# Late fused weights, scaled plain weights beside the experts, and other cyclic orders in a two-layer cross-attention and MoE kernel

## The reference, cut to what matters

```python
# layer 0
x = x + cross_attention(layernorm(x), ctx)            # 16 heads of 16, masked
xn = layernorm(x)
probs = softmax(xn @ w_switch + b_switch); e = argmax # 8 experts, one per token
keep = (position of the token in its expert) <= 512   # capacity
x = x + gate * (relu(xn_e @ w1[e] + b1[e]) @ w2[e] + b2[e])
# layer 1
h = cross_attention with biases (layernorm(x), ctx); ffn W1, W2 ; h = x + ...
nodes[-1] = layernorm(h)
for c in 0..5:                                        # a cell of six attention nodes
    q, k, v = (src @ We[edge]) * ew[c] @ Wq/Wk/Wv[c]  # 8 heads of 32
    nodes[c] = nodes[c-1] @ We[edge] * ew + attention(q, k, v) @ Wo[c] * act_w[c]
out = h + layernorm(nodes[5]) * ln_g + ln_b
```

## Time and profile before

| | |
|---|---|
| median of 3 runs | 4257.91 us (4254.85 to 4258.33) |
| the profiled execution's own time | 4261.87 us |
| its span | 4260.1 us |
| mean granted TensorE clock | 0.978 |
| PE busy | 4052.2 us, 95% |
| DVE, ACT, POOL busy | 59%, 62%, 42% |

### The profile page before, as it was taken

How to read it: one execution, slowest core, us unless ns; L and a number is a source line. 1 busy time by engine, 2 the same in 40 slices (tenths; PEclk the granted TensorE clock), 3 DMA queues, 4 the chain that set the end, 5 groups by cost and what they waited for, 6 DMA issues and landing times.

```text
span 4260.1 us, 100693 instructions
## 1 busy us (share of the span) xinstructions
PE 4052.2 (95%) x38276; PEld 3431.3 (81%) x38276; DVE 2515.5 (59%) x6280; ACT 2647.2 (62%) x11818; POOL 1774.9 (42%) x1883
## 2 busy tenths in 40 slices
PE   8889998995999999999999999999999999999997
PEld 7778876664788888888888888888888888888885
DVE  6778883103566666566666666566666666666553
ACT  7778881112666666666666666666666666666663
POOL 4566662002344444444444444444444444444332
PEclk9999998997999999999999999999999999999998
DMA  4122214321000000000000000000000000000000
GB/s 161 55 66 74 63 52 140 110 71 51 14 14 14 14 14 13 13 13 14 20 15 14 14 13 12 12 12 12 12 12 12 12 12 19 11 14 11 4 4 6
DMA packets 117867, 129.75 MB, mean 30 GB/s; under 512 B 12006, under 2 KB 110676, under 8 KB 117264
## 3 DMA queue, kind: packets, MB, share of 16 engines
q1 hardware_dynamic: 105648, 109.80, 8.2%
q0 software_dynamic: 6144, 8.43, 0.7%
q10 hardware_dynamic: 5600, 5.07, 0.4%
HBM read 89.68 MB, written 41.94 MB: 31 GB/s over the span
## 4 chain that ended last, share of the span: by engine, by line
PE 58%; DVE 9%; ACT 5%; POOL 3%; issue 1%; DMA 0%; SPq 0%; POOLq 0%; DVEq 0%
PE c_product L1297 26%; PE c_product L1308 12%; PE c_product L1348 8%; PE c_scores L1338 6%; ACT c_front_probs L1118 4%; PE c_product L1371 4%; DVE c_neg_max L1173 2%; DVE c_xn L1158 2%; DVE c_routed L1158 1%; PE c_product L1359 1%; DVE c_x L1183 1%; POOL c_rstd L1064 1%; ACT c_probs L1118 1%; POOL c_probs L1076 1%; PE c_product L1285 1%
## 5 line engine op out<-in xcount | busy, mean ns | idle before, releaser
L1118 ACT ACTIVATE c_probs<-c_scores,c_neg_max 128x128 f32<-128x128 f32 x3072 | 1081.9, 407 | 480.5 <-DVE c_neg_max L1173 480.5
L1076 POOL TENSOR_TENSOR c_probs<-c_probs,c_row_inv 128x512 f32<-128x512 f32 x768 | 790.5, 1041 | 1211.3 <-DVE c_row_inv L1176 1208.7
L1297 PE MATMUL c_product<-c_nodes,cell_w 128*128 128x256 f32 x4352 | 1056.9, 383 | 2.7 <-DVE c_nodes L1164 1.0
L1297 PEld LDWEIGHTS c_product<-c_nodes,cell_w 128*128 128x128 f32 x4352 | 803.5, 190 | 124.8 <-issue 19.6
L1173 DVE TENSOR_REDUCE c_neg_max<-c_scores 128x4 f32<-128x512 f32 x1024 | 635.7, 683 | 254.9 <-PE c_scores L1338 254.9
L1118 ACT ACTIVATION_READ_ACCUMULATOR c_probs<-c_scores,c_neg_max 128x1 f32 x3072 | 757.7, 247 | 0.0
L1124 ACT COPY c_probsT<-c_product 128x512 f32<-128x512 f32 x768 | 413.3, 613 | 440.4 <-PE c_product L1348 440.4
L1308 PE MATMUL c_product<-cell_w,c_nodes 128*128 128x256 f32 x1792 | 435.4, 383 | 0.0
L1118 ACT ACTIVATE c_front_probs<-c_scores,c_neg_max 128x128 f32<-128x128 f32 x1024 | 358.3, 403 | 116.7 <-DVE c_neg_max L1173 116.7
L1348 PE MATMUL c_product<-consts_sb,c_probs 128*128 128x128 f32 x3072 | 398.8, 276 | 14.8 <-POOL c_probs L1076 13.7
L1348 PEld LDWEIGHTS c_product<-consts_sb,c_probs 128*128 128x128 f32 x3072 | 350.9, 142 | 47.8 <-POOL c_probs L1076 19.8
(11 more groups left out here) (157 smaller groups left out, 6540.7 us busy)
## 6 DMA issues: line engine op xcount, KB each, us to landing
e_w<-in_L_ffn_w SPq DMA_DIRECT2D x12, 1024.0 KB, 5.9
a_x<-in_x SPq DMA_DIRECT2D x32, 256.0 KB, 3.4
a_ctxT<-in_ctx_pairsT SPq DMA_DIRECT2D x32, 256.0 KB, 3.5
x<-a_x SPq DMA_DIRECT2D x32, 256.0 KB, 2.1
xn<-a_xn SPq DMA_DIRECT2D x32, 256.0 KB, 2.2
c_routed<-xn SPq DMA_DIRECT2D x32, 256.0 KB, 2.9
c_x<-x SPq DMA_DIRECT2D x32, 256.0 KB, 3.0
c_ctxT<-in_ctx_pairsT SPq DMA_DIRECT2D x32, 256.0 KB, 2.7
```

What stands on the lines that cost most here:

```text
L1076: nc.gpsimd.tensor_tensor(e, e, rinv[:, i, r].unsqueeze(2).broadcast_to([P, 4, T]), ALU.mult).then_inc(norm_made, 1)
L1118: a = nc.scalar.activation(probs(n)[:, r, k], S[r][:, k], ACT.Exp, bias=nmax[:, i, r, k:k + 1], accum_out=rsum[:, i, r, k:k + 1])
L1297: i = T_.matmul(m[:, u], w[:, k, u * P:(u + 1) * P], src[:, k], start=n == 0, stop=n == last)
```

## The change

It has five parts.

1. Only `F0` to `F5` stay in the first layer. `F6` to `F17` (nodes 2 to 5) move into the second layer's first turn, with a ring of four inputs that lies in buffers of nodes 3 to 5, loaded by ACT (the first four) and SP (the others).
2. `w.s` leaves POOL's first-layer queue. The plain weights are loaded by SP behind each expert's `w2`, and scaled by POOL in the experts' phase.
3. The second layer's loads: rows of job 0 first on SP, then `wk`, `wq`, `wv`; the rest on ACT. Each first use waits for its own load. In the experts' phase DVE copies the first rows before it waits for `b2`.
4. Other cyclic orders in the first layer, with `ROW_RING` 6 for 8 and `put:8` for `put:9`.
5. Other cyclic orders in the second layer.

```diff
 FIRST_PE_ORDER = """
-K:0 Tx:0 T0.0:1 S1:1 Q:0 Tn:3 O:2 L:3 T1.0:1 T0.1:1 S0:0 T1.1:1 V:0 A:1 r.n:4
+L:4 Q:1 T0.0:2 T0.1:2 S0:1 T1.0:2 T1.1:2 V:1 r.n:4 K:0 A:2 Tn:3 Tx:0 S1:1 O:2
 FIRST_DVE_ORDER = """
-nm:0 S0.i1:1 A^:2 K^:0 S0.i2:1 Tx^:0 S0.i3:1 r.n^:5 S1.x0:1 S1.x1:1 S1.x2:1 S1.x3:1 S1.i0:1 Q^:0 Tn^:3 r.oh:4
-S1.i1:1 O^:2 S1.i2:1 L^:3 r.sh:3 st1:2 S1.i3:1 nm1:2 mk:-1 st:-1 S0.x0:0 S0.x1:0 S0.x2:0 S0.x3:0 S0.i0:0 V^:0
+S0.i0:2 K^:1 S1.x2:2 Tx^:1 S1.x1:2 S1.x3:2 S1.x0:2 O^:3 S1.i1:2 Q^:1 L^:4 r.sh:4 S1.i2:2 S1.i0:2 st1:3 r.oh:4
+S1.i3:2 S0.x3:1 S0.x1:1 S0.x2:1 mk:0 st:0 nm1:3 S0.x0:1 r.n^:4 V^:1 nm:0 S0.i3:1 A^:2 Tn^:3 S0.i2:1 S0.i1:1
 FIRST_ACT_ORDER = """
-S0.e2:1 S0.e3:1 r.ex:4 K^O:0 T0^0:1 T0^1:1 S1.e0:1 S1.e1:1 S1.e2:1 S1.e3:1 T1^0:1 T1^1:1 T0^2:1 T0^3:1 T1^2:1
-T1^3:1 S0.e0:0 S0.e1:0
+K^O:1 S1.e2:2 S1.e1:2 S1.e0:2 S1.e3:2 r.ex:4 T0^0:2 T0^1:2 T0^2:2 T0^3:2 T1^1:2 T1^0:2 T1^2:2 S0.e3:1 T1^3:2
+S0.e1:1 S0.e2:1 S0.e0:1
 FIRST_POOL_ORDER = """
-S0.n1:1 S0.n2:1 S0.n3:1 S1.n0:1 S1.n1:1 S1.n2:1 w.s:6 rs1:2 S1.n3:1 put:9 rs:-1 S0.n0:0
+S1.n0:1 S1.n2:1 S1.n3:1 rs1:2 rs:-1 put:8 S0.n3:0 S0.n0:0 S0.n2:0 S0.n1:0 S1.n1:0
...
-    X_RING, ROW_RING, GROUP = 4, 8, 4
+    X_RING, ROW_RING, GROUP = 4, 6, 4
...
-            for n in range(RING, len(fused)):
-                if n == 2 * RING:
-                    store(JOBS - 1)
+            for n in range(RING, FUSED_FIRST):
                 sp.wait_ge(prod, n_prod[f"B{n - RING}", JOBS - 1])
                 fuse_load(n)
+            store(JOBS - 1)
...
 # phase_experts, SP, behind the load of w2[e]
+                if e <= NODES:
+                    sp.dma_start(cell["w"][:, e - 1, EDGE], ...).then_inc(plain_in[e - 1], 16)
+                    sp.dma_start(cell["w"][:, e - 1, OUT], ...).then_inc(plain_in[e - 1], 16)
 # phase_experts, DVE
+            rows_turned(0)
             dve.wait_ge(b2_in, 16)
-            rows_turned(0)
...
 PE_ORDER = """
-f.Tx:0 T0.1:1 S3:2 f.K:0 f.Q:0 K4:2 K1:1 A0:1 f.Sb0:0 T3.0:2 O0:1 f.V:0 T3.1:2 Q1:1 f.Tb0.0:0 A3:2 S1:1 O3:2
-V1:1 K2:1 Q4:2 T1.0:1 f.Tb0.1:0 S4:2 T1.1:1 K5:2 V4:2 A1:1 f.Ab0:0 O1:1 T4.0:2 T4.1:2 f.Sb1:0 A4:2 Q2:1 O4:2
-f.Tb1.0:0 f.Tb1.1:0 S2:1 V5:2 f.Ab1:0 Q5:2 f.W1a:0 f.W1b:0 S5:2 f.W2:0 K3:1 T2.0:1 V2:1 f.Txn:0 T5.0:2 T2.1:1
-K0:0 T5.1:2 Q0:0 A2:1 A5:2 S0:0 V0:0 O2:1 O5:2 T0.0:0 Q3:1 V3:1
+S3:2 T0.1:1 f.Tx:0 f.K:0 V3:2 f.Q:0 A0:1 f.Sb0:0 K1:1 O0:1 T3.0:2 K4:2 T3.1:2 Q1:1 A3:2 f.Tb0.0:0 S1:1
+f.Tb0.1:0 V1:1 O3:2 K2:1 T1.0:1 Q4:2 T1.1:1 S4:2 f.V:0 K5:2 V4:2 A1:1 T4.0:2 f.Sb1:0 O1:1 f.Ab0:0 T4.1:2 Q2:1
+f.Tb1.0:0 A4:2 S2:1 f.Tb1.1:0 O4:2 f.Ab1:0 Q5:2 f.W1a:0 f.W1b:0 T2.0:1 S5:2 f.W2:0 K3:1 V2:1 T2.1:1 V5:2
+f.Txn:0 T5.0:2 T5.1:2 A2:1 Q0:0 A5:2 K0:0 O2:1 S0:0 O5:2 Q3:1 V0:0 T0.0:0
...
+LATE_FUSE_PE_PLACES = """
+start:0 F6 B6 F7 B7 F8 B8 F9 B9 F10
+f.Tx:0 B10
+f.Q:0 F11
+f.Sb0:0 B11 F12 F13 B12 B13 F14
+f.Tb0.0:0 B14
+f.Ab0:0 F15 F16 B15
+f.Tb1.0:0 B16 F17
+f.Tb1.1:0 B17
...
+            load_rows(0)
+            load_context(0)
+            for t, a, got in ((wk, ...), (wq, ...), (wv, ...)):
+                sp.dma_start(t[:], halves(io[a])).then_inc(got, 16)
+            fuse_load(FUSED_FIRST + LATE_RING)
+            load_rows(1)
+            for n in range(FUSED_FIRST + LATE_RING + 1, len(fused)):
+                fuse_load(n)
```

More of the change, by code:

```diff
@@ L64, in cell_plan, with fused_weights @@
     return plan
+def fused_weights(plan):
+    return [(c, k, plan[c]["edge"][k]) for c in range(NODES) for k in (TO_Q, TO_K, TO_V)]
 def unfold(table, jobs):
@@ L71, in unfold, with with_fused @@
     return [(name, k - s) for k in range(min(first, 0), jobs + last) for name, s in order if 0 <= k - s < jobs]
+def with_fused(order, table, job_of, at):
+    order = list(order)
+    for line in table.strip().splitlines():
+        behind, *pieces = line.split()
+        name, k = behind.split(":")
+        i = 0 if name == "start" else order.index((name, job_of(int(k)))) + 1
+        order[i:i] = [(p, at) for p in pieces]
+    return order
 def counted(order, test):
@@ new lines @@
+f.Sb1.n2:0 f.Sb1.n3:0 S2.n0:1 S2.n1:1 S2.n2:1 S2.n3:1 S5.n0:2 S5.n1:2 f.rs3:0 S5.n2:2 S5.n3:2 f.x3b:0 S0.n0:0
+S0.n1:0 e.rs:2 S0.n2:0
+"""
+LATE_FUSE_PE_PLACES = """
[7 more added lines that the diff above has]
+f.Tb1.1:0 B17
+"""
+LATE_FUSE_DVE_PLACES = """
+start:0 F6^ B6^ F7^
+f.x2:0 B7^
+f.st:0 F8^ B8^
+f.x:0 F9^ B9^ F10^
+f.Tx^:0 B10^
+f.Q^:0 F11^
+f.x2:1 B11^
+f.Sb0.i1:0 F12^
+f.Sb0.i3:0 B12^ F13^ B13^
@@ L909, in phase_second_layer @@
+f.x:1 F14^ B14^
+f.Sb1.i0:0 F15^
+f.Ab0^:0 F16^
+f.Sb1.i2:0 B15^
+f.Sb1.i3:0 B16^ F17^ B17^
+"""
+def phase_second_layer(nc, io, scratch, keep, cell, cst, out):
     ctx = io["ctx_pairsT"]
@@ L1312, in node, with weights_landed @@
                 return nd[:, s, SLOT_OF[c]]
+            def weights_landed(c, k, j):
+                f = fused.index((c, k, plan[c]["edge"][k]))
+                if j == 0 and f >= FUSED_FIRST:
+                    landed(f"F{f}", 0)
             def node_landed(c, j):
@@ L1396, in _ @@
                     project_rows(product(n, j), (w2, hid), between=lambda: landed("f.W1b", j)).then_inc(prod, 1)
+                elif n[0] == "F":
+                    r = int(n[1:]) % LATE_RING
+                    pe.wait_ge(late_in[r], 32 * ((int(n[1:]) - FUSED_FIRST) // LATE_RING + 1))
+                    project(product(n, j), late[r]).then_inc(prod, 1)
+                elif n[0] == "B":
+                    c, k, edge = fused[int(n[1:])]
+                    m, we = product(n, j)[:, 0], late[int(n[1:]) % LATE_RING][1]
+                    for o in range(2):
+                        for h in range(2):
+                            i = T_.matmul(m[:, o:o + 1], we[:, h, o * P:(o + 1) * P], be[:, h, edge:edge + 1],
+                                          start=h == 0, stop=h == 1)
+                    i.then_inc(prod, 1)
                 elif n == "O5":
```

204 lines of the change are left out of this document (117 added, 87 removed).

## The result

The changed kernel takes 4282.18 us (median of 4 runs, 4279.10 to 4286.11) beside 4257.22 us (4254.85 to 4258.33) for the kernel before: a ratio of 1.0053, 95% interval 1.004 to 1.0066. It is slower by 25 us; the forecast was 4308 us, 50 more than before. The profiled execution is one of 4282.18 us, with a span of 4280.4. One execution of a later run, the profiled one of putrs, took 11035 us, and nothing is compared with it.

A forecast was written before the change was run, and what follows sets the result against it. PE's own work was taken to bound the steady second layer, with DVE the next limit in the first. Terms 107 - 26.5 + 4 - 5.8 + 2 - 31 = +50 on 4261.87 gave 4311.6, as median 4308 us; range 4260 to 4385.

The forecast's parts named there:

- +107: First layer, 23 turns to job 31: 24.5 us a turn, so 563.5 instead of 456.3 us.
- The clock price of 1.0 us a turn: First layer's 23 turns: PE's clock drops after each stop, taken as 1.0 us a turn, between 0 and 3.4.
- The stop: First layer, DVE ahead of `nm1`: still for 5.9 us a turn during root, two puts and a 3.3 us landing.
- The share hidden: First layer's turn with the wait: 21.8 us if other idle vanished, 25.0 if nothing hid it; middle taken, 23.5.
- DVE's busy time as a floor: First layer: DVE's 15.9 us of work a turn plus the wait, 21.8 us, as the shortest turn.
- the rival of the hidden wait: First layer: the wait falls into DVE's existing idle time, a turn is 21.8 us, whole 4246; chance 0.17.
- Twelve fused weights: First layer's end: without them the experts' first transfer comes at about 692.3, -26.5 us.
- PE's wait for the inputs of `F3`: First layer's drain: inputs issued only after `nm1` of job 30, PE waits about one landing, +4 us (0 to 8).
- The plain weights: First layer: scaling leaves POOL's queue, 24.3 us go, 8.1 before job 8, 16.2 after; cost beside the experts nothing.
- the swap: Experts' start: rows copied without waiting for `b2`, hidden layer starts at 726.1 instead of 731.90, -5.8 us.
- The head: Second layer's head: twelve fused weights, 32 us of work, lie mostly in 40 us of idle PE; +2 us, -6 to +15.
- The second layer: Second layer's new order: `f.Txn` stall goes, -1.0 us a turn (-1.6 to +1.0), 31 turns, -31 us.

The follow-up runs named there:

- putrs: The changed kernel with put:8 one place earlier, ahead of rs:-1, in POOL's first-layer order, on the second chip: 4251.11 us, ratio 0.9956.
- ring8: The changed kernel with eight row buffers in the first layer (ROW_RING 8 for 6), nothing else: 4199.23 us, ratio 0.9862.
- put7: The changed kernel with put:7 for put:8 in POOL's first-layer order, ring of six kept: 4196.70 us, ratio 0.9856.
- putrs2: The changed kernel with put:8 ahead of rs:-1 in POOL's first-layer order, run again on the third chip: 4251.89 us.
- l1old: The changed kernel with the first-layer orders and fused-weight places of the kernel before, eight row buffers, put:9, without w.s: 4176.25 us, ratio 0.9807.
- fuse18: l1old with all eighteen fused weights made at the first layer's end, none in the second layer's head: 4220.04 us on the second chip.
- swapback: l1old with the experts' start of the kernel before, DVE waiting for b2 ahead of the first rows' copies: 4212.15 us on the second chip.
- l2old: The changed kernel with the four second-layer orders of the kernel before, two fused-weight lines on DVE displaced: 4336.12 us, ratio 1.0188.
- l1old7: l1old with a ring of seven row buffers for eight, on the third chip: 4335.27 us, ratio 1.0147.
- after2: The changed kernel as it is, run again on the third chip: 4311.31 us.

## Why the prediction was right and wrong

The direction, the mechanism and its place were right: 23 stops on DVE ahead of the normalisation, behind `st`, made of root, two puts and a landing, and gone in two different ways (ring8, put7) with 83 and 85 us of the whole. What was mis-sized is one term of the sum, "**+107**" for the 23 turns: measured +78.9, a turn of 23.27 us for 24.5.

- *The clock price of 1.0 us a turn* (23 of the 28 us) was the failed step: "after a stop of 3.14 us PE lost some 3.4 us in a 7 us stretch". Without it the forecast turn would have been 23.5, 540.5 us for the 23; measured 535.2. The clock did fall, to 0.94 from 0.98 in ring8, and PE's busy time rose by (438.94 - 413.98) / 23 = 1.1 us a turn. But this can't be added to the stop as it was. If the whole 1.1 were on the path, 2.2 of the 3.3 us would be the stop's and 3.1 of the stop would be hidden; then the stop of 2.93 us in putrs2, where PE's busy time rose by 0.16 a turn (417.64 for 413.98), would have cost 0.2 us, and it cost 0.55 to 0.63. If instead what exceeds the slack is paid in full, at most 0.4 us a turn is left for the clock. PE had 4.2 us of idle time in each turn (96.3 / 23); that the slower work lay in it fits, and was not shown by itself.
- *The stop*, forecast 5.9, was 5.26 in the mean. The landing of a put was taken at 3.3 us from the earlier trace rows; in the turn shown the put that counts landed 2.39 us after its start, and the median for all puts of the changed kernel in this stretch is 2.4, for ring8 3.6 (issues and landings below). Why the same put lands later where nothing stops for it was not tried. By the Trainium skill ("DMA: Bandwidth & Descriptors", section "Anatomy of one DMA — SWDGE (gpsimd) path") the estimate was 2.3 us for the landing and 4.9 for the stop. This turn's 2.39 and 4.96 agree with it, while the mean stop, 5.26, lies between that and the forecast. That the 4285 which the sum had by it is 3 us from the result is luck: it still holds 23 us for the clock, and its old pace is 19 us too low.

```profile
buf<-a_xn,slots POOLq DMA_INDIRECT x46, 2.4
```

```profile
buf<-a_xn,slots POOLq DMA_INDIRECT x48, 3.6
```

- *The share hidden*, the middle of 21.8 and 25.0, came out nearly right by luck, by errors that cancel. The old pace of 19.14 was the wrong foot: without the wait the new order stands at 19.97 (ring8), the old one at 19.14 (l1old). Against these 0.8 us, the stop is 0.6 shorter, and 2.0 to 2.4 us of it are hidden, where the middle had 1.5.
- *DVE's busy time as a floor* (15.9 us a turn) was too high: 337.3 us, 14.7 a turn, mainly since the normalisation at L450 took 407 ns for one instead of 637. So the rival of the hidden wait could have gone lower than I allowed. It didn't happen: 2.0 to 2.4 us of the stop are hidden, not the 4 that DVE stood idle in each turn before (91 / 23).
- *Twelve fused weights*: -21.3 with the wait for `F3`, forecast -22.5; the move alone took 24.8 (fuse18). The sum is right partly by luck. The prediction has no stop for `nm1` of jobs 29 to 31, as no `st` stands ahead of it; but it waits for its put all the same, and these stops cost 7.4 us (79.2 for 71.8 in ring8). Without them the new order would have stood at -28.7. PE's wait for the inputs of `F3`, forecast 4, was 5.7 (2.1 in ring8), and is part of them.
- *The plain weights*: 22.6 us gone, forecast 24.3. Next to nothing came back in the experts' phase: with the old start it is 245.4 us long (swapback) beside 244.9 before. In the changed kernel it is 4.3 us shorter, and that is the swap, forecast -5.8. Right.
- *The head* is right in sum, -1.3 for +2, and its parts were not as I had them: the twelve cost 7.3 us (fuse18), and with the old order l2old's head is 14.5 us longer than that of before (165.0 against 150.5). What gave this back in the changed kernel, the new order or the two displaced lines, is open. PE stood still until the first pair of weights, which I had not in the sum:

```profile
1023.73 3.78 PE L1382 MATMUL c_product<-c_probsT 128*128 128x256 f32 x8 [9.19 <-DMA c_probsT<-in_L_ffn_Wq]
```

- *The second layer*: forecast -31, measured -32.6 with the last turn. `f.Txn` has no stall any more, as stated ahead. No new stall is seen, since PE's idle time is 2.9 us in 2953. But PE's busy time rose by 0.4 us a turn (982.72 for 978.99 in ten turns), which is the size I had given to four more changes between full and quarter tiles (0.1 each); that it is these changes was not tried apart.

What would show it, point by point: DVE idle 5 to 6 us ahead of the old L456, 23 times: yes, released by "issue" and not by the transfer. K's copies 24 to 25 us apart: no, 21.5 to 22.9 in most ordinary turns and 25.5 to 27.4 in those with routing, 23.27 in the mean. PE near 70% with a clock below 0.95: 82%, 0.94. The experts' first transfer near 805: at 777.3. The hidden layer 7 us after it: 8.0.

## What to carry to other kernels

A cyclic order with a ring has one distance that decides: between the place where a slot's last reader is issued and the place where the slot is written again. Check it across the engines' tables: here one digit of a table (`put:7`) or two more buffers is worth 83 and 85 us. Here a stop cost what exceeded the slack of its cycle, and the clock that fell with it cost, by the reckoning above, at most 0.4 us a turn where 1.0 had been added; so price stop and clock together from one cycle with such a stop, where there is one, before you add them. When a change has several parts, look at each alone: here the new second-layer order, the moved weights and the earlier start were all gains (the other places of the second layer's loads were not tried alone), and the kernel with them and the old first-layer order is 1.9% faster than the kernel before.

## What the runs showed of the hardware that was not expected

- DVE's normalisation of 128x256 with two per-partition operands took 637 ns for one in the kernel before (and 639 in l1old) and 407 in the changed kernel (414 in ring8), with operands and lines the same. In the new order POOL runs none of its strip normalisations at that place in the turns looked at (about 484 to 509 us). One kernel shows both times: in l1old7 the pair behind the stop, with POOL idle, takes 0.74 us, and the next pair, beside a normalisation of POOL, 1.03. That POOL's work is the cause was not tried by itself. DVE's lines of the kernel before and after, for jobs 8 to 31, and then the two pairs of l1old7:

```profile
L456 DVE TENSOR_SCALAR a_xn<-a_x,a_mean_var,a_rstd 128x256 f32<-128x256 f32 x92 | 55.0, 637 | 35.3 <-POOL a_rstd L349 35.3
```

```profile
L450 DVE TENSOR_SCALAR a_xn<-a_x,a_mean_var,a_rstd 128x256 f32<-128x256 f32 x92 | 33.6, 407 | 121.0 <-issue 121.0
```

```profile
437.35 0.74 DVE L447 TENSOR_SCALAR a_xn<-a_x,a_mean_var,a_rstd 128x256 f32<-128x256 f32 x2 [6.00 <-DMA buf<-a_xn,slots]
...
442.16 1.04 POOL L364 TENSOR_TENSOR a_probs<-a_probs,a_row_inv 128x512 f32<-128x512 f32 x1 [1.46 <-DVE a_row_inv L474]
...
442.64 1.03 DVE L447 TENSOR_SCALAR a_xn<-a_x,a_mean_var,a_rstd 128x256 f32<-128x256 f32 x2
```

- The same kernel's second-layer turn took 98.2 us in the first profile and 99.0 on the third chip, at a full clock both times. Ten turns compared by instruction (983.67 and 992.05 us) differ by 8.4 us: PE is busy for 5.7 us more (988.45 for 982.72) and idle for 2.7 more. Of its groups of matmuls only the front's scores differ, 41.3 us for 34.2 (records of neighbours overlap); no other differs by more than 0.3. PE's waits of after2 list 26 stops at the scores with no releaser. Why, is open. The whole of the kernel before was 16.6 us longer on that chip, that of the changed one 29.1.

```profile
PE c_scores L1431 <- issue: 7.0, 26, 0.3
```
